# Attention loop of an adaLN block on one core: window values ahead of the query transposition, half of the projection last, and another order on ScalarE and VectorE

## What is computed

```python
h = _layernorm(x) * (1 + ca) + sa                 # x: 2 x 1024 x 512
x = x + ga * attn(h)
h = _layernorm(x) * (1 + cb) + sb
x = x + gb * ffn(h)                               # 1408 wide, weights as integers with a scale

# attn: H = 16 heads, D = 128, window of 128 keys, one compressed key for 16 tokens
q = rmsnorm(apply_partial_rope(h @ Wq_c @ Wq_up))
k_sw = rmsnorm(apply_partial_rope(h @ Wk)); v_sw = h @ Wv
ck = rmsnorm(h.reshape(b, nb, M * HID) @ W_comp)
c_out = attend(q @ ck.T * scale, valid, sink, ck)
sw_out = attend(CAP * tanh(q @ k_sw.T * scale / CAP), sw_mask, sink, v_sw)
attn = ((c_out + sw_out) grouped @ Wg) @ Wo
```

## Time and profile before

| | before |
|---|---|
| median of 3 runs | 1065.0 us (1063.42 to 1066.18) |
| profiled execution | 1067.07 us, its span 1065.2 us |
| mean granted clock of TensorE | 0.952 |
| TensorE busy | 949.0 us (89%), 4782 matmuls |
| VectorE busy | 678.3 us (64%) |
| ScalarE busy | 565.4 us (53%) |
| GpSimd busy | 559.0 us (52%) |

### The profile page before, as it was taken

How to read it: one execution, slowest core, us unless ns; L and a number is a source line. 1 busy time by engine, 2 the same in 40 slices (tenths; PEclk the granted TensorE clock), 3 DMA queues, 4 the chain that set the end, 5 groups by cost and what they waited for, 6 DMA issues and landing times.

```text
span 1065.2 us, 16048 instructions
## 1 busy us (share of the span) xinstructions
PE 949.0 (89%) x4782; PEld 787.0 (74%) x4782; DVE 678.3 (64%) x1262; ACT 565.4 (53%) x1554; POOL 559.0 (52%) x758
## 2 busy tenths in 40 slices
PE   5776889569999999999999999999558999999996
PEld 5776757457888888888788888888346777878784
DVE  1764355458888888888888888888267533242312
ACT  1563343157777777777777787777131322324221
POOL 0263000168888888888888888886113222222221
PEclk9898888769999999999999999999769999999998
DMA  7547741320323123131132312310180010020101
GB/s 239 172 156 263 294 149 60 119 60 28 122 55 107 45 55 122 55 106 45 55 122 55 107 46 55 121 35 11 60 354 1 1 64 16 1 79 1 41 1 41
DMA packets 52595, 93.66 MB, mean 88 GB/s; under 512 B 9905, under 2 KB 29361, under 8 KB 49713
## 3 DMA queue, kind: packets, MB, share of 16 engines
q1 hardware_dynamic: 41904, 64.52, 19.0%
q10 hardware_dynamic: 10624, 28.26, 7.5%
HBM read 75.33 MB, written 26.08 MB: 95 GB/s over the span
## 4 chain that ended last, share of the span: by engine, by line
PE 40%; issue 14%; POOL 12%; DVE 10%; ACT 2%; DMA 1%; ACTq 1%; POOLq 1%; DVEq 0%; SPq 0%
PE banks L919 23%; PE banks L1425 7%; PE banks L1390 4%; POOL gus L1567 3%; PE banks L959 2%; PE banks L988 2%; PE banks L935 2%; POOL qn L1227 1%; DVE pcS L1124 1%; PE banks L968 1%; DVE qn L1141 1%; POOL pc L1234 1%; POOL rq L1208 1%; DVE banks L1108 1%; DVE ws L1158 1%
## 5 line engine op out<-in xcount | busy, mean ns | idle before, releaser
L919 PE MATMUL banks<-fold,aoT 128*128 128x512 f32 x768 | 194.2, 402 | 1.4 <-DVE aoT L1093 1.4
L1425 PE MATMUL banks<-hT,w_hi 128*128 128x512 f32 x704 | 175.7, 401 | 4.0 <-DVE hT L1504 2.6
L919 PEld LDWEIGHTS banks<-fold,aoT 128*128 128x128 f32 x768 | 140.6, 190 | 29.4 <-DVE aoT L1093 1.9
L1567 POOL TENSOR_TENSOR gus<-arena,gus 128x512 fp32r<-128x512 f32 x44 | 61.2, 1391 | 191.5 <-ACT gus L1468 191.5
L1425 PEld LDWEIGHTS banks<-hT,w_hi 128*128 128x128 f32 x704 | 132.8, 191 | 36.9 <-DVE hT L1504 4.2
L919 PE MATMUL banks<-k_st,qT 128*128 128x320 f32 (+6 forms) x768 | 123.3, 310 | 0.0
L1537 DVE SCALAR_TENSOR_TENSOR arena<-banks,sg,arena 128x512 f32<-128x512 f32 x44 | 33.0, 750 | 128.6 <-ACT arena L1463 128.6
L919 PEld LDWEIGHTS banks<-k_st,qT 128*128 128x128 f32 x768 | 109.6, 192 | 0.2
L1463 ACT ACTIVATE arena<-banks,sg 128x512 f32<-128x512 f32 x44 | 30.4, 690 | 142.6 <-PE banks L1425 142.6
L1390 PE MATMUL banks<-w_hi,gus 128*128 128x512 f32 x352 | 91.3, 401 | 11.8 <-POOL gus L1567 9.6
L919 PE MATMUL banks<-pp,v_st 128*128 128x512 f32 x360 | 99.7, 411 | 0.0
(11 more groups left out here) (174 smaller groups left out, 2008.0 us busy)
## 6 DMA issues: line engine op xcount, KB each, us to landing
arena<-in_wq_blocks ACTq DMA_DIRECT2D x8, 1056.0 KB, 4.9
wq_words<-in_wq_blocks ACTq DMA_DIRECT2D x8, 1056.0 KB, 7.0
w_lo<-wq_words SPq DMA_DIRECT2D x11, 768.0 KB, 15.4
go_raw<-in_w_go SPq DMA_DIRECT2D x16, 512.0 KB, 7.3
arena<-in_L_attn_h SPq DMA_DIRECT2D x16, 256.0 KB, 8.3
comp_raw<-in_w_comp SPq DMA_DIRECT2D x16, 256.0 KB, 5.5
v_parts<-v_out ACTq DMA_DIRECT2D x4, 1024.0 KB, 4.6
k_st<-k_parts SPq DMA_DIRECT2D x32, 128.0 KB, 2.6
```

Of the source, the lines that this page charges most:

```text
L919: last = pe.matmul(out, lhs[a], rhs[b], start=start and q == 0 and u == 0, stop=stop and q == n - 1 and u == 2)
L1425: last = pe.matmul(GU[2 * (n % 2) + w][:], parts[a][:, h, cols], hT[:, c % 2, x, k], start=(k == 0 and q == 0), stop=(k == KC - 1 and q == ...
L1567: pool.tensor_tensor(gus[:, n % 2, 1], gu[:, n % 2], gus[:, n % 2, 0].bitcast(F32), ALU.subtract).then_inc(gu_lo, 1)
```

## The change

The lists of three engines are put in another order, and the reciprocal of `compressed_sum` becomes an operation of its own, `compressed_reciprocal`, which stands behind `query_low`. No instruction is added or left out in a full step.

```diff
         steps(pe, (0, query), (3, transpose_probs), (2, scores), (3, transpose_compressed), (4, project_first),
-              (4, project_second), (1, transpose_query), (3, window_values), (3, compressed_values), alone=EVERY)
+              (3, window_values), (1, transpose_query), (3, compressed_values), (4, project_second), alone=EVERY)
...
-        steps(act, (4, out_high), (3, probs_high), (0, weight_squares), (0, squares), (3, compressed_high), (2, tanh), (2, exp),
-              (1, query_high), (2, compressed_exp), (2, over_sum))
+        steps(act, (4, out_high), (3, probs_high), (0, squares), (3, compressed_high), (0, weight_squares), (2, tanh), (2, exp),
+              (2, compressed_exp), (1, query_high), (2, over_sum))
...
         def compressed_sum(g):
             wait(dve, "c_exp", g.n())
             dve.tensor_reduce(csm[:, g.slot], cs[:, g.slot], AX.X, ALU.add).then_inc(s["c_sum"], 1)
+
+        def compressed_reciprocal(g):
             wait(dve, "c_sum", g.n())
             wait(dve, "c_nrm", g.n(2))
             dve.reciprocal(crs[:, g.slot], csm[:, g.slot]).then_inc(s["c_rec"], 1)
...
-        steps(dve, (4, out_low), (5, tile_out), (3, probs_low), (2, compressed_logits), (2, merge), (3, masked_low),
-              (3, compressed_low), (2, compressed_max), (2, window_sum), (0, scale_query), (1, query_low), (2, compressed_sum),
+        steps(dve, (5, tile_out), (4, out_low), (3, probs_low), (3, masked_low), (2, compressed_logits), (2, merge),
+              (2, compressed_max), (3, compressed_low), (0, scale_query), (2, window_sum), (2, compressed_sum), (1, query_low),
+              (2, compressed_reciprocal),
               alone=EVERY)
```

## The result

| | before | after |
|---|---|---|
| median | 1065.11 us (4 runs, 1063.42 to 1066.18) | 1096.83 us (4 runs, 1096.2 to 1097.59) |
| ratio, 95% interval | | 1.0303 (1.0289 to 1.0318) |
| profiled execution, span | 1067.07, 1065.2 us | 1096.2, 1093.7 us |
| mean granted clock | 0.952 | 0.959 |
| 52 full steps of the attention, each | 8.25 us | 8.88 us |

The change makes the kernel 31.7 us slower. Forecast were 1105 us and slower at 88%.

What follows compares the result with a forecast made beforehand. TensorE's 8.09 us of work plus 0.16 idle a step was taken as the bound. 52 steps x (8.99 - 8.25) = 38.5, batch starts +1.5 and +1, the rest 0: together +41, so 1105 us median, range 1078 to 1114.

Steps and rivals of the forecast that it cites:

- The row that decides: VectorE's `masked_low`, 1.24 us where it meets GpSimd's `masked_high` against 0.69 alone, ending 1.84 after that one's start: one after the other.
- The loop of 8.99: Chain through GpSimd and VectorE from one `masked_high` to the next, summed to 8.99 us a step after the change, 7.84 before.
- Where it settles: `masked_high` was to start 2.6 us into each step, 0.3 ahead of `masked_low` at 2.90, so the collision repeats.
- X: Start of GpSimd's `masked_high`, counted from the step's query projection on TensorE; forecast to settle at 2.6 us.
- the step lasts X + 6.4: TensorE's step length from the start of `masked_high`: `compressed_low` ends 3.93 later, some 0.1 reaction, then 2.34 to the next query projection.
- the rival in which VectorE gets in first: `masked_low` starts before `masked_high`, window values wait until 4.85, step 8.46 us: 1078 us, slower by less; 12%.
- TensorE's waits: The wait before the transposition of `pc` vanishes; 0.85 us a step appears ahead of the query transposition.
- The window values find both parts: TensorE's window values, wanted at 4.48 us of a step, would find both masked parts done at 4.47.
- Edits at nothing: Moves of `tile_out`, `weight_squares`, `compressed_exp` and the reciprocal of `compressed_sum` on VectorE and ScalarE, claimed to cost nothing.
- the clock is no term: The granted clock was to add nothing: 1.00 at the second batch's start, though TensorE waited up to 1.11 us a step.
- the forecast case: Collision in each step, loop between 8.8 and 9.1 us: 1105 us, own range 1094 to 1113; kept 70%.
- The faster rival: The two masked parts run side by side, TensorE's 8.09 us are the step: 1054 us; 9%.

## Why the prediction was right, point by point

**The row that decides.** Right, and tested in both directions: the 1.24 us row stood for all later collisions in which GpSimd is first. Each ends 1.84 behind the start of `masked_high`, GpSimd's follower is held up too, and with one operand in PSUM the instruction takes 0.687 us (median) in all 64 groups. One reading was wrong: the 0.69 us row at 421.56 does not run alone. Beside it GpSimd's `rsqrt` takes 1.54 us where it has 1.02 in the earlier trace rows:

```profile
421.58 1.54 POOL L1208 TENSOR_TENSOR rq<-rq,exponent 128x4 f32<-128x4 f32 x1
```

So the kernel before pays for the collision too, on GpSimd's side: `rsqrt` takes 1.33 to 1.54 us in 27 of its 64 groups, and never over 1.02 once the mask lies in PSUM. What that costs the kernel before was not tried.

**The loop of 8.99.** Right to 0.06 in the step shown (8.93); the mean over 52 steps is 8.88 since the logits are narrower in the earlier tiles of a batch (from their start to that of `merge` it is 0.17 us early in a batch and 0.33 at its end, where 0.27 stood). 52 x 0.62 = 32.3 came, for 38.5 forecast. Part 3 of the change, `scale_query` ahead of `window_sum`, was priced about right for full steps: 0.14 of the 0.2.

**Where it settles.** X came out at 430.15 - 427.32 = 2.83, not 2.6. What failed in size is "the step lasts X + 6.4": from the start of the query transposition TensorE needed 2.11 (425.21 to 427.32), not 2.34, its transposition and compressed values taking 0.39 and 0.35 instead of 0.56 and 0.46. In the step shown `masked_high` starts 421.22 - 418.39 = 2.83 behind the query projection and VectorE asks at 2.92, a margin of 0.1, not 0.3. GpSimd came first in all full steps but the first one or two of a batch, mostly by 0.08 to 0.18, so the forecast held by less than the text said; the rival in which VectorE gets in first was nearer than 12% suggests, and in the kernel before with `masked_low` moved it does so in part of the steps.

**TensorE's waits.** The one for `pc` went in the full steps but the first few of a batch (idle time put down to it in the whole span: 10.5 us before, 6.0 after); the one ahead of the query transposition came, 0.63 on average (36.6 us in 58 steps) where 0.85 stood. "The window values find both parts" was wrong: they waited 0.40 to 0.50 in nearly all steps, 28 us in all. The end of `masked_low` was put right, but TensorE starts only 0.23 behind it. For the total it made no difference, since that wait is taken out of the later one; as a mechanism of its own it was missed. Alone, TensorE's order costs 16 us, which the forecast held for nothing; that it did not show in the changed kernel is the longer loop's doing, which no sentence of the forecast foresaw. There it was luck.

**Edits at nothing.** Right for ScalarE's list, by its own run. `tile_out` and the later reciprocal of `compressed_sum` were not tried alone.

**The ends of the attention.** Forecast were +1.5 and +1 for the batch starts and 0 for drain and rest; measured +1.3, -1.2 and -3.9. Of the last, 2.3 are in the drain, from the last query projection to the check of the weights (763.07 - 724.32 = 38.75 before, 793.16 - 756.74 = 36.42 after). Two things make them. The last window values now stand ahead of half of a projection (1.3 us). And "the clock is no term" was wrong there: from 751 to 755 us the kernel before had a mean granted clock of 0.57, after TensorE had idled 1.71 us, and the 12 products of a projection took 4.17 us instead of 2.60; the changed kernel idled as long in the same place and kept 1.00 throughout its drain. Against them stands a `pc` that comes 0.6 later in the drain. Around the first batch's start the clock differs as well (mean granted 0.70 from 222 to 239 us before, 0.90 after); how much of the -1.2 that makes was not separated. The other 1.6 of the -3.9 lie behind the drain, and nothing here tells their cause. Together with the steps (32.3 against 38.5, -6.2) these make the 12 us by which +41 was too much against +28.5. So a part of what brought the measured time under the forecast was no term of it.

**Numbers.** 1096.83 lies inside 1078 to 1114, and inside the forecast case's own 1094 to 1113. The faster rival did not come. The rule of the Trainium skill's page Advanced Engine Details and Errata, section VectorE Performance Modes, that two-port instructions of VectorE and GpSimd's block each other, is not the whole of it here: `masked_low` is in none of them by the Trainium skill's page VectorE: DVE Perf Modes, section Why `tensor_tensor` can't do 2×_2P or 4×, and took 0.87 us or more in each of the 64 groups of the changed kernel, 1.56 on average, where it takes 0.69 undisturbed. The Trainium skill's page SBUF — State Buffer, section Who interferes with whom, names two SBUF inputs as a case of its own; the run with the mask in PSUM agrees, 0.687 us beside a running GpSimd instruction.

## What to carry to other kernels

Before an instruction of VectorE with two SBUF operands is put next to one of GpSimd that becomes ready at the same time, look for one place in the old trace where the two overlap: its length is the price, and everything queued behind it on VectorE pays too. Look at the GpSimd instructions beside it as well: where VectorE's is at its usual length, GpSimd's may be the longer one. In the changed kernel, moving one operand to PSUM took the collision away and gave more (35 us) than undoing any one edit did (18 at most); under the lists of before with `masked_low` moved it gave back what that move had cost, and no more. In a software pipeline, write each loop down as a sum from one instruction to its own next start, through every engine it crosses: the longest loop decides, shorter ones add nothing, and an edit that looks harmless next to it (TensorE's order here) can be the second longest, which is felt as soon as the first is repaired.

## What the runs showed of the hardware

- The collision goes both ways: in the changed kernel GpSimd's 0.20 us `square_sum` takes 0.65 while `masked_low` runs, its `masked_high` 1.75 instead of 1.29 where VectorE is first, and in the kernel before its `rsqrt` up to 1.54 instead of 1.02. And 1.75 instead of 0.68 was seen for the attention's only other VectorE instruction with two SBUF operands, the batch's mask, when it met `add_tile` (524.03 to 525.33):

```profile
524.13 1.75 DVE L1158 TENSOR_TENSOR prob<-prob,kons 128x512 f32<-128x512 f32 x1
```

- TensorE started 0.23 us behind the end of `masked_low` in nearly all steps that waited for it, for an instruction with five waits, but 0.07 behind `compressed_low`, for one with three. I had taken 0.05 to 0.1 for both. Why they differ was not tried.
- After a wait, TensorE's four loads of the query transposition take 0.39 until the next group starts, without one 0.56, also where the order of TensorE is the old one. So a wait there costs 0.17 us less than its length.
